# Source one-hots of the second gather stage: from one wide VectorE compare to ScalarE distances and a rectifier

## The chip, the cores and the metric

One core of a Trainium2 chip runs the whole program. The metric is the device time of one execution in microseconds (us). The times are those of the kernel before and after on the same kind of core; a profile is one execution of its own.

## What is computed

The reference takes 6250 nodes with 256 values and 100000 edges (src, dst). What matters here is the graph layer and what stands behind it:

```
xn = layernorm(x)
agg = segment_sum(xn[nbr], dst, 6250); cnt = segment_sum(1, dst, 6250)
x = x + (xn @ W1.T + b1 + (agg / max(cnt, 1)) @ W2.T + b2) + mix(xn)     # mix: per head of 32: q @ (k^T v / N), k and v normalized xn
x = x + ffn(layernorm(x))                                                 # 8 experts, one per node, capacity 977
```

(The call passes edge_index = stack(src, dst), so rows are summed by src and fetched by dst.)

## The kernel before, in words

The edges are sorted on the chip into tiles of 128 edges, by block of 128 nodes. For each tile, GpSimd's L511 issues one indirect DMA, which gathers 128 rows of 1 KB (a high and a low fp16 part of the projected node) out of the DRAM tensor xn_parts into a ring of 32 slots (the SBUF tensor w). TensorE then sums a tile into nodes by two matmuls (L764 with the high part and a column of ones, L765 with the low part) against a one-hot matrix S of 128 edges by 128 nodes: S[p, n] = 1 where edge p belongs to node n of the block. VectorE's L1018 adds the PSUM result to the block's sums in XA.

There are two gather stages. The first has T0 = 392 tiles, one block each; beside it the second chunk of edges is sorted (VectorE and ScalarE). The second stage has 438 dense tiles; a tile that holds a boundary between blocks is summed once for each block, which makes 486 items. The queues in it:

- GpSimd (L502 to L512) has nothing but gathers. For a gather of the second stage it waits until SyncE says that the slot 32 tiles back is free (s_free, L469); SyncE says so when the last item of that tile was summed.
- SyncE (L459 to L469) counts landed tiles (s_land, L461), and TensorE waits for that count before an item (L758).
- TensorE: `sum_tile(t)` (L743) waits for the landing, at each eighth item for the one-hots (s_S), and for the adding of the item four back (s_ev). Between items stand the products of the heads (L826; items 16 to 287, behind VectorE and ScalarE steps that `heads` orders), and, from item 288 on, one "own" part for each of 49 blocks, four items apart: transposes (L838), then products with W1 and the bias (L844, L846).
- VectorE: `tile(t)` (L1003) adds an item (L1018). The one-hots of eight tiles are one instruction, `source_onehots` (L995 to L999), half a group ahead. S has 16 tiles, so two groups. Between items stand the head statistics (L1301 to L1322), `key_values` (L1327) ahead of item 288, and the two additions of each own block (L1361, L1364).
- ScalarE (L599 to L627): Square and Sqrt for each of 17 head batches (L601, L603), then for each own block a copy of XA (L620, which TensorE's transposes wait for), a copy of the transposes (L623), and a DMA of x (L613).

The block ends when all queues are through; then come `nodes` (L1378, normalization, routing, scatter to expert rows) and `experts` (L1625).

The line that the change takes out of the second stage:

```
v.tensor_tensor(S[:, ...8 tiles...], iota_1 (broadcast over 8 tiles), srcl[:, t:t + SB] (broadcast over 128 nodes), ALU.is_equal)
```

Of the kernel before, what the change touches and what calls it, by code (L numbers as in the profile page):

```python
# [5 lines left out]
ALU = mybir.AluOpType  # L6
ACT = mybir.ActivationFunctionType
AX = mybir.AxisListType
F32 = mybir.dt.float32
F16 = mybir.dt.float16  # L10
# [6 lines left out]
P = 128  # L17
N, D = 6250, 256
NB = -(-N // P)
LASTROWS = N - (NB - 1) * P  # L20
LD = 4
HD = 3
# [16 lines left out]
SR, SB = 16, 8  # L39
AR = 4  # L40
KR, KR1 = 8, 12
# [32 lines left out]
T0 = CHUNKS[0][3]  # L74
DENSE = -(-COLS1 * EP // P)
ITEMS = DENSE + NB - 1
IW = -(-ITEMS // SB) * SB
AHEAD = 16
WMAX = max(c[1] for c in CHUNKS)
TMAX = max(T0, IW)  # L80
# [5 lines left out]
HEAD0, KV_AT = 1, 1 + NB // HD + 1  # L86
OWN0 = KV_AT
# [156 lines left out]
def edges(nc, ctx, kk, dram, x, src, dst, w1t, w2t, gb1, gb2, kw, kb, vw, vb, gate_w, gate_b):  # L244


    def sb(name, shape, dt):
        return ctx.enter_context(nc.sbuf_tensor(name, shape, dt))

    def sem(name):  # L250
        return ctx.enter_context(nc.semaphore(name))
# [3 lines left out]
    XA, ident, upper, upinc, ones, eps = (kk[n] for n in ("XA", "ident", "upper", "upinc", "ones", "eps"))  # L255
    W1, W2, brow, gw, gb = (kk[n] for n in ("W1", "W2", "brow", "gw", "gb"))
    bank = kk["psum"]
    psV, psP, psG, psQ = bank[2:4], bank[4], bank[5:7], bank[7]
# [12 lines left out]
    iota_1 = sb("iota_1", [P, P], F16)  # L271
# [39 lines left out]
    LH = sb("LH", [P, KR * P], F16)  # L311
    LV = sb("LV", [P, KR * 2 * P], F16)
    HT = sb("HT", [P, KR * TMAX], F16)
# [5 lines left out]
    assert KR1 == KR + 4 and LB == 4 and 12 * P + 4 * TMAX <= 4 * LD * D  # L319
    DI = HT[:, :].bitcast(I32)  # L320
    idx = sb("idx", [P, T0 + CHUNKS[1][3]], I32)
    srcl = sb("srcl", [P, T0 + IW], F16)
    buck = sb("buck", [1, T0 + IW], I32)
    lanes = sb("lanes", [P, 6], F32)
    starts = sb("starts", [P, 4], F32)
# [3 lines left out]
    keep = v2[:, 0:IW // 2].bitcast(F16)  # L329
# [5 lines left out]
    pick = [HT[:, n * TMAX:n * TMAX + IW] for n in range(4)]  # L335
    assert IW // 2 <= COLS0 and CHUNKS[1][3] <= 4 * P and IW // 2 <= EC - IW
    S = sb("S", [P, SR * P], F16)
    xT = [S[:, n * 4 * D:(n + 1) * 4 * D].bitcast(F32) for n in range(2)]
    spare = [G2[:, n * GW:n * GW + 2 * D] for n in range(GR)]
    hv = sb("hv", [P, 2 * 2], F32)  # L340
# [24 lines left out]
    s_S, s_tile, s_ev = sem("source_onehot"), sem("tile_summed"), sem("tile_added")  # L365
# [13 lines left out]
    s_past = sem("past_a_wait")  # L379
    s_ts, s_tr, s_trc, s_si, s_sid, s_rows = (sem(n) for n in (  # L380
        "sources_by_lane", "sources_turned", "sources_by_tile", "sources_picked", "item_sources", "item_rows_ready"))
    s_land, s_free = sem("tiles_landed"), sem("tiles_free")

    block = ctx.enter_context(nc.Block())
# [130 lines left out]
    def _(act):  # L515
# [80 lines left out]
                ins = act.activation(value_slot(k, n), lane_slots(k, 1), ACT.Copy, scale=v[0:EP, COLS0 + k:COLS0 + k + 1])  # L596
            ins.then_inc(s_lv, 1)

        def heads(m, nb):  # L599
            act.wait_ge(s_cen, m + 1)  # L600
            act.activation(sqr[:, 0:nb * D], cen[:, 0:nb * D], ACT.Square).then_inc(s_sq, 1)  # L601
            act.wait_ge(s_ss, m + 1)
            act.activation(hq[:, 0:nb * HEADS], hq[:, 0:nb * HEADS], ACT.Sqrt, scale=1.0 / (HC - 1)).then_inc(s_hstd, 1)  # L603
        with act.Fori(0, NB // HD) as m:
            heads(m, HD)
        heads(NB // HD, 1)
        act.wait_ge(s_kv, 1)

        def again(b):
            if b >= LD:  # L610
                act.wait_ge(s_x0, b - LD + 1)
            rows = P if b < NB - 1 else LASTROWS
            act.dma_start(xr[b % LD][0:rows, :], x[b * P:b * P + rows, :]).then_inc(s_xr[b % LD], 16)  # L613

        for b in range(2):
            again(b)

        def own(b, h):
            act.wait_ge(s_xt, b + 1)
            act.activation(xs[:, h * D:(h + 1) * D], XA[:, xcols(b)], ACT.Copy).then_inc(s_xs, 1)  # L620
            act.wait_ge(s_xt, b + 3)
            act.wait_ge(s_xp, b + 1)
            act.activation(xts[:, h * D:(h + 1) * D], psV[h][:, 0:D], ACT.Copy).then_inc(s_xtc, 1)  # L623
        for b in range(NB):
            own(b, b % 2)
            if b + 2 < NB:
                again(b + 2)  # L627

    @block.tensor
    def _(pe):  # L630
# [112 lines left out]
        def sum_tile(t):  # L743
            if t == 0:
                pe.wait_ge(s_one, 2)
            if t < T0:
                o = slot(t)
                pe.wait_ge(s_g[t % RING], 16 * (t // RING + 1))
            else:
                i = t - T0  # L750
                if i % GR == 0:
                    many = min(GR, ITEMS - i)
                    item[:] = [nc.values_load_multi_w_load_instructions(
                        row[:, i:i + many], engines=[mybir.EngineType.PE], min_val=low, max_val=high,
                        skip_runtime_bounds_check_because="an item's tile is one of the DENSE tiles, its slot one of the ring")[1]
                        for row, low, high in ((item_slot, 0, (RING - 1) * GW), (item_need, 1, DENSE))]
                o = item[0][i % GR]
                pe.wait_ge(s_land, item[1][i % GR] & 511)  # L758
            if t % SB == 0:
                pe.wait_ge(s_S, t // SB + 1)  # L760
            if t >= AR:
                pe.wait_ge(s_ev, t - AR + 1)
            lhs = S[:, t % SR * P:(t % SR + 1) * P]
            pe.matmul(psA[t % AR][:, 0:AGW], lhs, ring_high[:, ds(o, AGW)], start=True, stop=True)  # L764
            pe.matmul(psA[t % AR][:, 0:D], lhs, ring[:, ds(o, D)], start=False, stop=True, skip_group_check=True).then_inc(s_tile, 1)  # L765
# [109 lines left out]
    def _(v):  # L875
# [83 lines left out]
        n = NB // (2 * LD)  # L959
# [43 lines left out]
        def tile(t):  # L1003

            if (t if t < T0 else t - T0) % GR == 0:
                many = min(GR, (T0 if t < T0 else T0 + ITEMS) - t)
                offsets[:] = nc.values_load_multi_w_load_instructions(
                    buck[0:1, t:t + many], engines=[mybir.EngineType.DVE], min_val=0, max_val=(NB - 1) * RW,
                    skip_runtime_bounds_check_because="the place step clamps the tiles' blocks to NB - 1")[1]
            if t in (0, T0):  # L1010
                source_onehots(t)
            if t % SB == SB // 2 and t + SB // 2 not in (T0, T0 + IW):
                source_onehots(t + SB // 2)
            v.wait_ge(s_tile, t + 1)
            if t:
                v.wait_ge(s_ev, t)
            o = offsets[(t if t < T0 else t - T0) % GR]
            v.tensor_tensor(XA[:, ds(o, AGW)], XA[:, ds(o, AGW)], psA[t % AR][:, 0:AGW], ALU.add).then_inc(s_ev, 1)  # L1018
# [151 lines left out]
        def decode_dense():  # L1170

            tiles = CHUNKS[1][3]
            v.wait_ge(s_sx, 2)
            a, b, d, e = (DI[:, n * TMAX:n * TMAX + tiles] for n in range(4))
            v.tensor_copy(a, psV[0][:, 0:tiles])
            step(v.tensor_copy(b, psV[1][:, 0:tiles]))
            v.memset(lane_src[:, tiles:4 * P], 0.0)
            v.tensor_copy(ident16, ident[:, :])
            wait()
            v.tensor_scalar(d, a, 3, None, ALU.logical_shift_left)  # L1180
            step(v.tensor_scalar(e, b, 8, None, ALU.logical_shift_right))
            wait()
            step(v.tensor_scalar(a, b, 255, None, ALU.bitwise_and))
            v.tensor_tensor(idx[:, T0:T0 + tiles], d, e, ALU.bitwise_or).then_inc(s_dec, 1)
            wait()
            v.tensor_copy(lane_src[:, 0:tiles], a).then_inc(s_ts, 1)
            for _ in range(GAP):
                yield
            v.wait_ge(s_ts, 1)
            for n in range(4):  # L1190
                v.tensor_scalar(pick[n], item_tile, lanes[:, 2 + n:3 + n], None, ALU.is_equal)
            v.wait_ge(s_tr, 1)
            v.tensor_copy(src_lane, psG[0][:, 0:4 * P]).then_inc(s_trc, 1)
            step(v.tensor_scalar(item_slot, item_tile[0:1, :], float(1 + T0 % RING), None, ALU.add))
            v.tensor_scalar(item_need, item_tile[0:1, :], 2.0, None, ALU.add)
            v.tensor_copy(tile_used, used16[0:1, :])
            wait()
            step(v.tensor_scalar(item_slot, item_slot, RING - 1, None, ALU.bitwise_and))
            wait()
            step(v.tensor_scalar(item_slot, item_slot, float(GW), None, ALU.mult))  # L1200
            for _ in range(GAP):
                yield
            wait()
            v.sem_inc(s_rows, 1)
            v.wait_ge(s_si, 1)
            v.tensor_tensor(srcl[:, T0:T0 + IW], psG[1][:, 0:IW], keep, ALU.mult).then_inc(s_sid, 1)
            v.wait_ge(s_sid, 1)

        after_mask = {16: lambda: pair_stats(0), 24: lambda: pair_scale(0), 28: largest,
# [149 lines left out]
        def own(b):  # L1359
            v.wait_ge(s_xp, b + 3)  # L1360
            v.tensor_tensor(XA[:, xcols(b)], XA[:, xcols(b)], psG[b % 2][:, 0:D], ALU.add).then_inc(s_xa, 1)  # L1361
            v.wait_ge(s_xr[b % LD], 16 * (b // LD + 1))
            v.wait_ge(s_xa, b + 3)
            v.tensor_tensor(XA[:, xcols(b)], XA[:, xcols(b)], xr[b % LD], ALU.add).then_inc(s_x0, 1)  # L1364
# [465 lines left out]
```

## Time and profile before

| what | us |
|---|---|
| median of 3 runs (lowest to highest) | 1998.8 (1995.85 to 1999.64) |
| the profiled execution's own time | 1998.75 |
| its span, first to last instruction | 1997.1 |
| first gather of the first stage (L511) | 305 |
| first gather of the second stage | 836.57 |
| last gather | 1412.93 |
| first instruction of `nodes` | 1421.83 |

Busy time is a share of the span over stages with different limits. Engines: PE is TensorE, PEld its weight loads, DVE VectorE, ACT ScalarE, POOL GpSimd, SPq SyncE's queue. PEclk is the granted clock of TensorE as a share of full speed. A busy POOL in a gather is GpSimd writing the descriptors of one indirect DMA, and not the transfer.

### The profile page before, as it was taken

How to read it: one execution, taken by the hardware profiler on the slowest of the kernel's cores; microseconds unless marked ns; L12 is line 12 of the kernel's file. 1: busy time of each engine (PE TensorE's matmuls, PEld its weight loads, DVE VectorE, ACT ScalarE, POOL GpSimd, SP SyncE). 2: the span in 40 equal slices, each digit the busy share in tenths (PEclk: the TensorE clock that was granted, in tenths of full speed). 3: DMA queues.
4: the chain of work that ended last, by engine and by line, in shares of the span. 5: the costliest groups of instructions: out<-in, count | busy, mean ns of one | idle time of the engine just before them, and what ended most of it. 6: DMA issues, size and time to landing. Idle time of an engine off the chain costs nothing. (4 is left out here: it accounts for less than half of the span.)

```text
span 1997.1 us, 27369 instructions
## 1 busy us (share of the span) xinstructions
PE 1529.7 (77%) x6558; PEld 885.3 (44%) x6558; DVE 1367.3 (68%) x3735; ACT 710.2 (36%) x1954; POOL 985.5 (49%) x969
## 2 busy tenths in 40 slices
PE   4599995667778777365665558798593999999997
PEld 2255542233333333133333335454482766666665
DVE  8998997889998988476666657666781433444344
ACT  4488890008787876000000002111281222222221
POOL 0000006777777777777777777777263111111111
PEclk7699997679999998555555558878655999999999
DMA  6980013333333333743333334444464123323200
GB/s 185 180 151 32 32 36 86 98 100 94 99 98 97 95 96 98 86 123 100 101 100 101 98 111 131 127 132 127 140 226 163 41 96 97 105 96 103 101 9 5
DMA packets 101500, 204.49 MB, mean 102 GB/s; under 512 B 19794, under 2 KB 64760, under 8 KB 99392
## 3 DMA queue, kind: packets, MB, share of 16 engines
q0 software_dynamic: 49488, 131.52, 23.6%
q1 hardware_dynamic: 43164, 64.16, 12.1%
q10 hardware_dynamic: 8700, 7.07, 1.2%
q8 instruction: 64, 1.05, 0.2%
q14 instruction: 84, 0.69, 0.1%
HBM read 157.43 MB, written 49.89 MB: 104 GB/s over the span
## 5 line engine op out<-in xcount | busy, mean ns | idle before, releaser
L511 POOL DMA_INDIRECT w<-xn_parts,idx x830 | 856.4, 1032 | 260.8 <-issue 236.4
L1018 DVE TENSOR_TENSOR XA<-XA,bank 128x257 f32 x878 | 367.3, 418 | 280.9 <-PE bank L765 250.1
L764 PE MATMUL bank<-w,S 128*128 (+1 forms) x878 | 294.0, 337 | 275.0 <-SPq L461 114.6
L764 PEld LDWEIGHTS bank<-w,S 128*128 128x128 f16 x878 | 93.4, 106 | 486.8 <-issue 301.1
L765 PE MATMUL bank<-w,S 128*128 (+1 forms) x878 | 298.2, 342 | 0.0
L1800 POOL DMA_INDIRECT out<-ob,tok x64 | 66.5, 1040 | 401.2 <-DVE ob L1786 384.9
L596 ACT ACTIVATE LV<-LH,v 125x128 f16<-125x128 f16 x600 | 182.5, 388 | 195.8 <-DVE LH L1268 195.5
L1724 PE MATMUL bank<-w,ht 128*117 128x256 f32 (+1 forms) x1024 | 223.7, 379 | 0.0
L1713 PE MATMUL bank<-xt,w 128*128 128x468 f32 (+1 forms) x512 | 214.8, 578 | 0.8 <-ACT xt L1738 0.8
L1748 ACT ACTIVATE ht<-bank,b1c 128x468 f32<-128x468 f32 (+1 forms) x128 | 85.6, 669 | 333.4 <-PE bank L1713 333.4
L1724 PEld LDWEIGHTS bank<-w,ht 128*117 128x117 f32 (+1 forms) x1024 | 188.8, 186 | 30.5 <-issue 0.4
L1777 DVE TENSOR_TENSOR y<-bank,b 128x256 f32<-128x256 f32 (+1 forms) x64 | 27.1, 424 | 234.5 <-PE bank L1724 234.4
L731 PE MATMUL bank<-HT,LV 125*128 125x440 f16 x600 | 151.5, 361 | 15.6 <-ACT LV L596 12.5
L489 POOL DMA_DIRECT2D xn_parts<-w x13 | 10.7, 826 | 281.4 <-DVE w L953 281.4
L1713 PEld LDWEIGHTS bank<-xt,w 128*128 128x128 f32 x512 | 97.9, 191 | 109.1 <-issue 106.6
L997 DVE TENSOR_TENSOR S<-iota,srcl 128x1024 f16<-128x1024 f16 x110 | 133.9, 1217 | 2.2 <-issue 2.2
L601 ACT ACTIVATE work<-work 128x768 f32<-128x768 f32 (+1 forms) x17 | 13.9, 817 | 330.5 <-DVE work L1307 330.5
L765 PEld LDWEIGHTS bank<-w,S 128*128 128x128 f16 x878 | 94.8, 108 | 33.9 <-issue 10.0
L590 ACT ACTIVATE LV<-LH,v 125x128 f16<-125x128 f16 x354 | 108.0, 391 | 3.0 <-DVE LH L1237 3.0
L596 ACT ACTIVATE work<-work,v 125x128 f16<-125x128 f16 x296 | 90.4, 388 | 24.7 <-DVE work L1268 24.5
L1273 DVE TENSOR_SCALAR HT<-iota_t,tf 125x440 f16<-125x440 f16 x300 | 94.9, 343 | 0.0
L725 PE MATMUL bank<-HT,LV 125*128 125x392 f16 x354 | 80.2, 336 | 11.3 <-ACT LV L590 6.7
(290 smaller groups left out, 2326.0 us busy)
## 6 DMA issues: line engine op xcount, KB each, us to landing
w<-f SPq DMA_DIRECT2D x16, 1024.0 KB, 7.6
w<-xn_parts,idx POOLq DMA_INDIRECT x830, 2.8
expert_rows<-XA SPq DMA_DIRECT2D x2, 6296.5 KB, 62.7
xb<-expert_rows SPq DMA_DIRECT2D x8, 1028.0 KB, 11.4
xb<-expert_rows SPq DMA_DIRECT2D x8, 939.7 KB
XA<-x SPq DMA_DIRECT2D x6, 1024.0 KB, 5.6
xn_parts<-w POOLq DMA_DIRECT2D x12, 512.0 KB, 3.3
work<-x ACTq DMA_DIRECT2D x48, 128.0 KB, 2.2
```

The costliest lines, as they stand in the source:

```text
L511: pool.indirect_dma_start(ring[:, o:o + 2 * D], None, tab, bass.IndirectOffsetOnAxis(ap=idx[:, t:t + 1], axis=0)).then_inc(s_g[t % RING], 16)
L590: ins = act.activation(value_slot0(col, n), lane_slots0(col, 1), ACT.Copy, scale=v[0:EP, col:col + 1])
L596: ins = act.activation(value_slot(k, n), lane_slots(k, 1), ACT.Copy, scale=v[0:EP, COLS0 + k:COLS0 + k + 1])
L731: ins = pe.matmul(psV[n][:, 0:CHUNKS[1][3]], value_slot(k, n), tile_slot(k), start=False, stop=False, skip_group_check=True)
L764: pe.matmul(psA[t % AR][:, 0:AGW], lhs, ring_high[:, ds(o, AGW)], start=True, stop=True)
L765: pe.matmul(psA[t % AR][:, 0:D], lhs, ring[:, ds(o, D)], start=False, stop=True, skip_group_check=True).then_inc(s_tile, 1)
L997: v.tensor_tensor(S[:, t % SR * P:(t % SR + SB) * P].rearrange("p (j n) -> p j n", n=P), iota_1[:, :].unsqueeze(1).to_broadcast([P, SB, P] ...
L1018: v.tensor_tensor(XA[:, ds(o, AGW)], XA[:, ds(o, AGW)], psA[t % AR][:, 0:AGW], ALU.add).then_inc(s_ev, 1)
L1273: v.tensor_scalar(tile_slot(k + j), iota_t[0:EP, 0:tiles], tf[0:EP, k + j:k + j + 1], None, ALU.is_equal).then_inc(s_ht, 1)
L1713: ins = pe.matmul(psH[f % 2][:, 0:cols], w1[q][:, k * F + f * P:k * F + (f + 1) * P], xt[n % 2][:, k * TQ * P:k * TQ * P + cols], start=(k ...
L1724: ins = pe.matmul(psY[m % 2][0:rp, 0:D], ht[:, f * TQ * P + m * rp:f * TQ * P + (m + 1) * rp], w2[q][:, f * D:(f + 1) * D], start=(f == 0) ...
L1748: act.activation(ht[:, f * TQ * P:f * TQ * P + cols], psH[f % 2][:, 0:cols], ACT.Relu, bias=b1c[:, e * FT + f:e * FT + f + 1]).then_inc(s_ ...
```

## The change

In the second stage the one-hots of a group of eight tiles are made by ScalarE: eight activations with Abs (iota_1 minus the tile's source, as a bias per partition, 128 columns each) into a buffer `far` in LH, four at a time, and one activation with Relu of 1 - |distance| over 1024 columns into S. VectorE writes the negated sources once, as fp32, in place of the fp16 ones (L1206). ScalarE's queue is written out anew: head steps, own steps, the half groups of distances and the one-hots alternate. The first stage keeps VectorE's one-hots.

```diff
+        def distances(j, half):
+            if j >= S1_GROUPS:
+                return
+            if half == 0 and j:
+                act.wait_ge(s_S1, j)
+            for n in range(half * SB // 2, (half + 1) * SB // 2):
+                ins = act.activation(far[:, n * P:(n + 1) * P], iota_1[:, :], ACT.Abs,
+                                     bias=less_src[:, j * SB + n:j * SB + n + 1])
+            ins.then_inc(s_far, 1)
+        def onehots(j):
+            if j >= S1_GROUPS:
+                return
+            act.wait_ge(s_far, 2 * j + 2)
+            act.wait_ge(s_tile, T0 + (j - 1) * SB)
+            o = (T0 // SB + j) * SB % SR * P
+            act.activation(S[:, o:o + SB * P], far, ACT.Relu, bias=ones[:, 0:1], scale=-1.0).then_inc(s_S1, 1)
-        with act.Fori(0, NB // HD) as m:
-            heads(m, HD)
-        heads(NB // HD, 1)
-        act.wait_ge(s_kv, 1)
-        for b in range(2):
-            again(b)
-        for b in range(NB):
-            own(b, b % 2)
-            if b + 2 < NB:
-                again(b + 2)
+        act.wait_ge(s_sid, 1)
+        for j in range(2):
+            distances(j, 0)
+            distances(j, 1)
+            onehots(j)
+        for g in range(max(S1_GROUPS // 2, OWN0 + -(-NB // LD))):
+            m, nb = g - HEAD0, HD if g - HEAD0 < NB // HD else 1
+            if g == KV_AT:
+                act.wait_ge(s_kv, 1)
+                for b in range(2):
+                    again(b)
+            for r in range(LD):
+                if HEAD0 <= g < KV_AT and r < 2:
+                    (squares, roots)[r](m, nb)
+                b = (g - OWN0) * LD + r
+                if g >= OWN0 and b < NB:
+                    own(b, b % 2)
+                    if b + 2 < NB:
+                        again(b + 2)
+                distances(2 * g + 2 + r // 2, r % 2)
+                if r % 2:
+                    onehots(2 * g + 2 + r // 2)
...
             if t % SB == 0:
-                pe.wait_ge(s_S, t // SB + 1)
+                if t < T0:
+                    pe.wait_ge(s_S, t // SB + 1)
+                else:
+                    pe.wait_ge(s_S1, (t - T0) // SB + 1)
...
-            if t in (0, T0):
+            if t == 0:
                 source_onehots(t)
-            if t % SB == SB // 2 and t + SB // 2 not in (T0, T0 + IW):
+            if t % SB == SB // 2 and t + SB // 2 < T0:
                 source_onehots(t + SB // 2)
...
-            v.tensor_tensor(srcl[:, T0:T0 + IW], psG[1][:, 0:IW], keep, ALU.mult).then_inc(s_sid, 1)
+            v.scalar_tensor_tensor(out=less_src, in0=psG[1][:, 0:IW], scalar=-1.0, in1=keep, op0=ALU.mult,
+                                   op1=ALU.mult).then_inc(s_sid, 1)
```

`squares` and `roots` are the two halves of the old `heads`; `own` and `again` are unchanged. There are 61 groups.

## Rows read from the trace of the kernel before

**Rows 1.** The page: busy time of each engine, and GpSimd's in 40 slices

```profile
PE 1529.7 (77%) x6558; PEld 885.3 (44%) x6558; DVE 1367.3 (68%) x3735; ACT 710.2 (36%) x1954; POOL 985.5 (49%) x969
...
POOL 0000006777777777777777777777263111111111
```

**Rows 2.** Windows: heads' part and own part of the second stage

```profile
core 0: us, PE busy (x) PEld busy (x) DVE busy (x) ACT busy (x) POOL busy (x), PEclk, DMA share, GB/s
860.00:1176.00 316.00, 190.03 (x744) 104.01 (x744) 211.03 (x432) 17.66 (x34) 243.18 (x240) 0.56 0.35 100
...
1192.00:1417.00 225.00, 190.44 (x788) 114.17 (x788) 141.57 (x320) 38.67 (x97) 170.81 (x169) 0.80 0.44 128
```

**Rows 3.** The chain that ended last: where it starts (start us, us, what)

```profile
1530.25 0.55 SPq L1666
```

**Rows 4.** Waits, 830 to 1420 us: GpSimd's (total, times, longest)

```profile
POOL w L511 <- SPq L469: 3.7, 12, 0.3
```

**Rows 5.** Line L511, 836 to 1414 us (duration ns min/median/max)

```profile
L511 POOL DMA_INDIRECT w<-xn_parts,idx x439: 942/946/1992, 835.3 to 1412.9; - x147
```

**Rows 6.** Timeline: end of the second stage (start us, us, what)

```profile
1412.93 1.06 POOL L511 DMA_INDIRECT w<-xn_parts,idx  x1 [0.30 <-issue]
...
1416.80 0.42 DVE L1018 TENSOR_TENSOR XA<-XA,bank 128x257 f32 x1 [0.39 <-PE bank L765]
1421.83 0.39 SPq L166 DMA_DIRECT2D w<-f  x1
```

**Rows 7.** Line L997, VectorE's one-hots, 836 to 1414 us

```profile
L997 DVE TENSOR_TENSOR S<-iota,srcl x61: 1215/1218/1283, 854.1 to 1406.8; 128x1024 f16<-128x1024 f16 x61
```

**Rows 8.** Timeline: one gather beside L1322, one beside L997

```profile
1002.39 0.95 POOL L511 DMA_INDIRECT w<-xn_parts,idx  x1 [0.30 <-issue]
1002.64 0.95 DVE L1322 TENSOR_TENSOR work<-work,hr 128x768 f32<-128x768 f32 x1
...
1005.35 1.22 DVE L997 TENSOR_TENSOR S<-iota,srcl 128x1024 f16<-128x1024 f16 x1
...
1006.15 1.25 POOL L511 DMA_INDIRECT w<-xn_parts,idx  x1 [0.30 <-issue]
```

**Rows 9.** Timeline: first and last of 65 slow gathers beside an L997

```profile
858.48 1.22 DVE L997 TENSOR_TENSOR S<-iota,srcl 128x1024 f16<-128x1024 f16 x1
...
859.08 1.45 POOL L511 DMA_INDIRECT w<-xn_parts,idx  x1 [0.30 <-PE bank L765]
...
1406.83 1.22 DVE L997 TENSOR_TENSOR S<-iota,srcl 128x1024 f16<-128x1024 f16 x1
1406.92 1.95 POOL L511 DMA_INDIRECT w<-xn_parts,idx  x1 [0.30 <-issue]
```

**Rows 10.** Groups by form, 860 to 1400 us (busy, mean ns | idle before, releaser)

```profile
L620 ACT ACTIVATE work<-XA 128x256 f32<-128x256 f32 x47 | 19.6, 417 | 20.6 <-DVE mcol L1357 20.4
L1364 DVE TENSOR_TENSOR XA<-XA,work 128x256 f32<-128x256 f32 x45 | 19.2, 426 | 5.0 <-DVE XA L1361 0.5
...
L1322 DVE TENSOR_TENSOR work<-work,hr 128x768 f32<-128x768 f32 x16 | 15.2, 953 | 0.0
L1307 DVE TENSOR_TENSOR work<-XA,hm 128x768 f32<-128x768 f32 x16 | 15.2, 951 | 0.0
...
L601 ACT ACTIVATE work<-work 128x768 f32<-128x768 f32 x16 | 13.5, 843 | 316.2 <-DVE work L1307 316.2
...
L601 ACT ACTIVATE work<-work 128x256 f32<-128x256 f32 x1 | 0.4, 416 | 14.2 <-DVE work L1307 14.2
```

**Rows 11.** Windows: 100 us of the first stage, columns as in Rows 2

```profile
500.00:600.00 100.00, 78.75 (x421) 35.27 (x420) 92.50 (x251) 80.72 (x268) 77.44 (x75) 0.98 0.35 99
```

**Rows 12.** Timeline: start of the second stage's sums

```profile
854.08 1.25 DVE L997 TENSOR_TENSOR S<-iota,srcl 128x1024 f16<-128x1024 f16 x1 [0.74 <-issue]
...
855.53 0.39 PE L764 MATMUL bank<-w,S 128*128 x1 [1.89 <-SPq L461]
```

**Rows 13.** TensorE's waits, 1200 to 1400 us (total, times, longest)

```profile
PE bank L764 <- SPq L461: 21.5, 25, 2.3
```

More of the change, by code:

```diff
@@ L321, in edges @@
     idx = sb("idx", [P, T0 + CHUNKS[1][3]], I32)
-    srcl = sb("srcl", [P, T0 + IW], F16)
+    srcl = sb("srcl", [P, T0], F16)
     buck = sb("buck", [1, T0 + IW], I32)
@@ L337, in edges @@
     S = sb("S", [P, SR * P], F16)
+    less_src = HT[:, 4 * TMAX:4 * TMAX + 2 * (IW)].bitcast(F32)
+    far = LH[:, 0:SB * P]
+    S1_GROUPS = (IW) // SB
+    assert 2 * (IW) <= 4 * TMAX and SB <= KR and T0 % SB == 0
     xT = [S[:, n * 4 * D:(n + 1) * 4 * D].bitcast(F32) for n in range(2)]
@@ L381, in edges @@
         "sources_by_lane", "sources_turned", "sources_by_tile", "sources_picked", "item_sources", "item_rows_ready"))
+    s_S1, s_far = sem("source_onehot_second"), sem("source_distances")
     s_land, s_free = sem("tiles_landed"), sem("tiles_free")
@@ L597, in _, with squares, roots @@
             ins.then_inc(s_lv, 1)
-        def heads(m, nb):
+        def distances(j, half):
[14 more added lines that the diff above has]
+            act.activation(S[:, o:o + SB * P], far, ACT.Relu, bias=ones[:, 0:1], scale=-1.0).then_inc(s_S1, 1)
+        def squares(m, nb):
             act.wait_ge(s_cen, m + 1)
             act.activation(sqr[:, 0:nb * D], cen[:, 0:nb * D], ACT.Square).then_inc(s_sq, 1)
+        def roots(m, nb):
             act.wait_ge(s_ss, m + 1)
             act.activation(hq[:, 0:nb * HEADS], hq[:, 0:nb * HEADS], ACT.Sqrt, scale=1.0 / (HC - 1)).then_inc(s_hstd, 1)
-        with act.Fori(0, NB // HD) as m:
-            heads(m, HD)
-        heads(NB // HD, 1)
-        act.wait_ge(s_kv, 1)
         def again(b):
```

## The prediction

> **What bounds the kernel now.** I read the page first, then the stage in windows, then GpSimd's waits and its line. The page says that no engine is busy throughout, and that GpSimd is busy in 77% of each slice over all of the two gather stages, flat, with one dip [rows 1]. A flat level under 100% is the sign of an engine with a fixed pause between instructions. The chain that ended last starts only at 1530 us, in `experts` [rows 3], so it says nothing of the gather stage; but the stages are in blocks that follow one another, and whatever the gather stage's end gains, all behind it gains. So the question is what ends the gather stage. Its last gather starts at 1412.93, the last sum is added at 1416.80, and `nodes` begins at 1421.83 [rows 6]: the stage ends 3.9 us after its last gather starts, which is little more than one landing and one item.
>
> GpSimd issues the 438 gathers without a break. Its longest wait for a free slot is 0.3 us, and that is also the pause between any two gathers, so it is never really held [rows 4, 6]. A gather takes 0.946 us in the median and at least 0.942, but up to 1.99 [rows 5]. 438 gathers at 0.946 + 0.30 would take 546 us; from 836.57 to 1412.93 they took 576. The 30.7 us between are gathers that were stretched. So the second stage is bound by GpSimd's descriptor writing, and the only thing in it that can be saved is these 30.7 us.
>
> Where do they come from? I went through the timeline gather by gather beside VectorE's. 74 gathers took over 1.00 us, and 65 of them overlap an L997, with 27.7 of the 30.7 us. The first is at 859.08 (1.45 us, L997 at 858.48), the last at 1406.92 (1.95 us, L997 at 1406.83) [rows 9]; a gather beside an fp32 instruction such as L1322 keeps its 0.95 us while one that meets the L997 at 1005.35 takes 1.25 [rows 8]. The windows agree without any pairing: 860 to 1176 holds 240 gathers in 243.18 us, 16.1 above 240 x 0.946, and the own part 169 in 170.81, 10.9 above [rows 2]. What is left, 3.0 us, lies beside L1322, L1364 and the like.
>
> **The change part by part.** *Removed from VectorE:* 61 one-hots of 1.218 us, 74.4 us [rows 7]. As VectorE's own time this is worth nothing: VectorE is busy 211 of 316 us and 142 of 225 [rows 2], and it isn't what ends the stage. What it is worth is the stretching: 27.7 us, or 0.454 us for each of the 61. The lowest bound is 0, if whatever replaces L997 stretches the gathers as much; the highest is all of 30.7.
>
> L997 is not the only VectorE instruction with two inputs in SBUF: L1322, L1307 and L1364 have 49.6 us of such time beside its 74.4 [rows 7, 10]. The rows speak for L997 alone, so the sum goes by 27.7; an even blame is rival 2. The page "GPSIMD Engine Reference" of the Trainium skill (8. Key points) stands for the even blame: GpSimd shares its SBUF interfaces with VectorE and contends with every VectorE instruction that runs in a two-port mode or has two SBUF inputs. By it the time would be that of rival 2, about 1982, and not 1973.
>
> *Added to ScalarE:* for each group eight activations of 128 columns and one of 1024. The near row for the former is the sorting's activations of 125 x 128 fp16 with a scale per partition, 268 in 80.72 us, 0.301 each back to back [rows 11]; eight are 2.4 us. For the latter the two forms of L601 give (843 - 416)/512 = 0.834 ns for a column and 1.06 us for 1024 [rows 10]. Both ends: 3.5 us for a group, and if the eight don't overlap and the three waits in a group cost 0.3 us each, 8 x 0.39 + 1.06 + 0.9 = 5.1 (0.39 is my estimate from 0.416 for 256 columns, less the 107 ns of 128 columns, and a margin of 80). A group's time will be 8/486 of about 549 us, 9.0 us. ScalarE's other work in the own part is 38.67 us in 225 [rows 2], 1.5 us a group. That makes 5.0 to 6.6 of 9.0: it fits, and no sum has a term for it. ScalarE works beside GpSimd in the first stage also, and 75 gathers took 77.44 us in 100 us with 80.72 of ScalarE's busy time [rows 11], 6.5 above 75 x 0.946, 0.087 for each, against 0.067 in the heads' part with ScalarE nearly idle (16.1 for 240), and VectorE has the fp16 compares of the sorting beside L997 there; and no gather of the second stage that met ScalarE alone took over 0.95.
>
> *Table loads:* Copy, Square and Sqrt already alternate in this stage without one, and Relu and Copy do in `experts`. I put 0. If Abs needed another table than Sqrt, 34 loads would lie in the heads' part, where ScalarE has 298 of 316 us free [rows 2]; the cover is large.
>
> *The first group comes later.* L997 at 854.08 let the first item start at 855.53 [rows 12]. Now 2.4 + 1.1 us on ScalarE stand there in place of 1.25, so the first item starts some 2.3 us later. Ahead of GpSimd lie 32 slots, and it is at gather 16 of the stage then; the lag is caught up before it needs slot 33. Price 0.
>
> *The order in ScalarE's queue.* This is the edit that can cost. The one-hots of group j + 1 wait until group j - 1 is all summed, and in the own part the next block's copy (L620, 0.417 us [rows 10]) stands behind them in the queue; TensorE's transposes wait for that copy, one item later. So once in every eight items TensorE may be held: Relu 1.06 + copy 0.42 + some 0.1, 1.6 us after the eighth item, less the item between. If TensorE is waiting for landings anyway, the next item ends some 1.4 us later and the stall is 0.2; if it has a backlog, the item takes 0.4 and the stall is 1.2. Does it have room? In the own part (24 groups) it is busy 190.4 of 225 us [rows 2] and waits 21.5 of 200 us for landings [rows 13], 24 over the part. The faster gathers take 10.9 of these, so 13 are left, 0.55 for a group, against a stall of 0.2 to 1.2. In the same part the adds no longer queue behind L997. Then there is `key_values`: ScalarE waits 20.4 us for it [rows 10], some 15 gathers pile up, and TensorE has the own part to work them off at a smaller surplus than now. I expect that it nearly does: I put the stage's end 2 us later behind its last gather than now, with 0 and 10 as the ends (10 being ten items not yet caught up at about 1 us each).
>
> *The conversion* at L1206 is one instruction for one. 0.
>
> **The sum.** On the profiled execution, 1998.75 (span 1997.1 and 1.65 around it; the median of the runs is 1998.8, the same): -27.7 for the gathers, +2 for TensorE's lag at the end: **1973.0 us**.
>
> **The rivals.**
> 1. *TensorE becomes the bound of the own part.* For it: busy 85%, and a stall that is 1.2 us a group once it lags, against 0.55 of room. The granted clock is 0.80 there [rows 2], so part of its work runs at 1.2 GHz, and stalls could keep it there. Against: a TensorE that lags is busy without a gap, and has finished its pile by 1250 us in this trace. If the own part doesn't get faster at all, its 10.9 us stay: 1982 to 1984. 17%.
> 2. *The stretching belongs to all VectorE instructions with two SBUF inputs alike*, and those that stay keep theirs, or take over what L997 had. L997 has 74.4 of 124.0 us of such time [rows 7, 10], 60%; 60% of 30.7 is 18.4, so 1998.75 - 18.4 + 2 = 1982. Against it are gathers of 0.95 us beside L1322 [rows 8]. 8%.
> 3. *Nothing moves*: ScalarE's reads and writes of fp16 stretch the descriptors as VectorE's did; 1998. Against it is the whole first stage. 3%.
> 4. *Slower: ScalarE's queue sets the pace of the own part.* One mechanism: Relu, the block's copy and the waits between stand in series with TensorE's transposes. The own part takes 225/24.75 = 9.1 us a group of eight now, with 7.7 of TensorE's work. The heads' part still gains 16 us, or 0.65 a group of the own part, so it decides from 9.75 on: from a stall of over 2.0 us a group. At 3 us, when distances too stand ahead of the copy, it is 10.7, 265 us for 225, 40 lost and 16 + 1 won: about 2022. 5%.
>
> My forecast has 67%, from 1969 to 1979. The range takes in the first two rivals: **1967 to 1984**. Faster by over 0.2% (4 us, about what a measurement can tell here): 0.92; within 0.2%: 0.03; slower: 0.05.
>
> **What the profile after would show.** The gathers of the second stage at 0.30 + 0.946 us, about 3 us above in all, the last starting near 1385; GpSimd still never held. No L997 behind 836 us, VectorE's share down by 74 us. ScalarE's eight near 2.4 us and Relu near 1.06. TensorE's transposes in the own part waiting for L620, some 0.2 to 1.2 us once in eight items, and the stage's last add 4 to 8 us behind the last gather. Everything from `nodes` on as long as before (1421.83 to the end, 575 us). It would be wrong if gathers are still stretched (rivals 2 and 3), or if the last gather starts on time but the last add comes over 10 us behind it, or GpSimd waits for slots (rivals 1 and 4).

## The result and the profile after

The changed kernel takes 1993.01 us (median of 20 runs, 1987.11 to 2000.83), the kernel before 1998.07 (20 runs): ratio 0.9974, 95% interval 0.9964 to 0.9984. It is faster by a quarter of a percent, where 1.3% was forecast; 1993 lies outside the forecast range of 1967 to 1984. The profiled execution took 1994.81, its span is 1993.2, and 575.8 us of it lie behind the gather stages as before (575.3). So what there is to explain lies in the second gather stage.

The page of the kernel after, against [rows 1]: VectorE has 62 us less, ScalarE 213 us more, and in slice 29 of 40 (1395 to 1445 us), where the stage ends, GpSimd is down from 2 to 0: its gathers are done before.

```profile
PE 1540.6 (77%) x6558; PEld 891.4 (45%) x6558; DVE 1305.0 (65%) x3674; ACT 922.9 (46%) x2503; POOL 964.0 (48%) x969
...
POOL 0000006777777777777777777777063111111111
```

The groups by form, 860 to 1410 us: what the one-hots cost ScalarE (busy us, mean ns). Four distances take 1.28 us back to back, the rectifier 1.15 (1.06 was worked out).

```profile
L611 ACT ACTIVATE LH<-iota,HT 128x128 f16<-128x128 f16 x456 | 143.2, 388 | 1.1 <-DVE XA L1407 0.3
...
L622 ACT ACTIVATE S<-LH,ones 128x1024 f16<-128x1024 f16 x58 | 66.6, 1148 | 131.8 <-PE bank L807 131.2
```

The window of the kernel after for the heads' part, columns as in [rows 2]:

```profile
860.00:1176.00 316.00, 193.01 (x748) 107.53 (x748) 177.10 (x404) 136.83 (x341) 241.38 (x246) 0.54 0.35 103
```

The heads' part has 246 gathers in 316 us for 240 before. For the own part I take the same work in each kernel, from the start of item 288 to that of item 480: the kernel before, the kernel after, and the one with the moved copy that is told of below.

```profile
1192.83:1410.52 217.69, 186.42 (x768) 112.00 (x769) 137.40 (x309) 38.28 (x96) 167.43 (x166) 0.79 0.44 129
...
1181.92:1411.18 229.26, 198.40 (x768) 118.73 (x769) 113.36 (x285) 118.37 (x303) 159.82 (x168) 0.75 0.43 125
...
1182.37:1392.36 209.99, 180.24 (x769) 108.59 (x770) 112.27 (x285) 115.60 (x303) 159.11 (x168) 0.82 0.47 135
```

The own part is 11.6 us longer than before, and TensorE is busy 12.0 us longer with the same matmuls, at a granted clock of 0.75 in place of 0.79. TensorE's waits in the kernel after, 1192 to 1410 us (total, times, longest):

```profile
PE bank L880 <- ACT work L640: 22.2, 22, 1.4
...
PE bank L806 <- SPq L466: 0.4, 1, 0.4
```

Over items 288 to 480 the kernel before has 23.4 us of waits for landings (in 200 us of it they are the 21.5 of [rows 13]). They are gone but for 0.4, and 22.2 us of waits for ScalarE's copy (L640) before the transposes (L880) are there: GpSimd isn't what TensorE waits for any more. All of TensorE's waits over 0.15 us add up to 37.8 us before and 37.5 after. So the stalls took the place of the waits for landings, and what lengthened the own part is the same matmuls at a lower clock: TensorE had 1.2 GHz, the lower of its two levels, for 115.1 us of it and for 90.4 before, and 24.7 us more at half the clock are 12.3 us of work. The end of the stage, against [rows 6]:

```profile
1391.67 0.95 POOL L516 DMA_INDIRECT w<-xn_parts,idx  x1 [0.30 <-issue]
...
1416.63 0.42 DVE L1060 TENSOR_TENSOR XA<-XA,bank 128x257 f32 x1
1417.33 0.39 SPq L166 DMA_DIRECT2D w<-f  x1
```

The stage in the profiles:

| us | before | after | moved copy (below) |
|---|---|---|---|
| first gather of the stage starts | 836.57 | 834.92 | 835.31 |
| from there to the last gather's start | 576.4 | 556.8 | 556.6 |
| from item 0 to item 276 (heads) | 313.2 | 307.6 | 306.2 |
| from item 288 to item 480 (own) | 217.7 | 229.3 | 210.0 |
| last gather's start to `nodes` | 8.9 | 25.7 | 8.8 |

The gathers gave 19.6 us. The stage's end, which now comes 25.7 us behind the last gather and not 8.9, gave 16.8 back. The stage also began 1.65 us sooner, so `nodes` starts 4.5 us sooner, and the span is 3.9 shorter.

### The profile page after: what moved, and what is told of

Read it like the earlier page. It is cut to its first block and busy times, and to the rows that moved or that the text cites. A ratio compares the mean times of both kernels' runs of the same rounds, so it can differ in the third digit from the quotient of the medians.

```text
span 1993.2 us, 27869 instructions
## 1 busy us (share of the span) xinstructions
PE 1540.6 (77%) x6558; PEld 891.4 (45%) x6558; DVE 1305.0 (65%) x3674; ACT 922.9 (46%) x2503; POOL 964.0 (48%) x969
## 5 line engine op out<-in xcount | busy, mean ns | idle before, releaser
L516 POOL DMA_INDIRECT w<-xn_parts,idx x830 | 834.8, 1006 | 260.8 <-issue 234.9
L611 ACT ACTIVATE LH<-iota,HT 128x128 f16<-128x128 f16 x488 | 153.0, 388 | 16.7 <-DVE HT L1248 15.6
L622 ACT ACTIVATE S<-LH,ones 128x1024 f16<-128x1024 f16 x61 | 70.0, 1148 | 173.8 <-PE bank L807 173.2
L601 ACT ACTIVATE work<-work,v 125x128 f16<-125x128 f16 x296 | 90.4, 387 | 23.3 <-DVE work L1311 23.1
```

Of the source, the lines that this page charges most:

```text
L516: pool.indirect_dma_start(ring[:, o:o + 2 * D], None, tab, bass.IndirectOffsetOnAxis(ap=idx[:, t:t + 1], axis=0)).then_inc(s_g[t % RING], 16)
L611: ins = act.activation(far[:, n * P:(n + 1) * P], iota_1[:, :], ACT.Abs, bias=less_src[:, j * SB + n:j * SB + n + 1])
```

## What held the gathers, row by row

Behind the result I paired every gather's start and length with VectorE's instructions more finely than in the forecast. Take the point 0.14 us after a gather's start. If a VectorE instruction with two inputs in SBUF runs at it, and began at least 0.18 us ahead of it (0.04 us ahead of the gather), the extra length of the gather is the end of that instruction less the point, within 0.02 us in all rows but one, which fits within 0.03. In the second stage of the kernel before, 66 gathers meet such an instruction with over 0.03 us still to run, and all are held. 9 more meet one that began 0.01 to 0.17 us ahead of the point (8 times L997), and none is lengthened. In the first stage 4 gathers are held by one that began so late, each time right behind an L1273 compare. Of the kernel after, a gather and the fp32 centring of the heads, no one-hot near:

```profile
1009.17 0.95 DVE L1350 TENSOR_TENSOR work<-XA,hm 128x768 f32<-128x768 f32 x1
1009.33 1.60 POOL L516 DMA_INDIRECT w<-xn_parts,idx  x1 [0.30 <-issue]
```

The instruction ends at 1010.12, the point is 1009.47, the hold 0.65: 0.946 + 0.65 is 1.60. The same sum gives, to 0.03 us, the 1.25 us of the gather at 1006.15 in [rows 8] (1006.57 less 1006.29 is 0.28), the 1.45 and the 1.95 of [rows 9], and it gives nothing for the gather at 1002.39 beside L1322, since that begins 0.25 us after the gather. Counted so, L997 holds 44 gathers of the kernel before by more than 0.03 us, for 20.1 us in all, L1307 12 gathers for 7.0, L1322 1.4, L1364 0.8. L1307 stood close ahead of L997, and the gather of both had been put down to L997. In the kernel after, 10.4 us are left of 30.1, 8.1 of them with the centring. Every gather there that is over 0.98 us long has a VectorE instruction at its point, so ScalarE's distances and rectifiers, new in this stage, hold none; that answers rival 3.

## The experiments

All kernels are changed from the kernel after (or before, where said), and each ratio is to the kernel before on the same chip. They ran on five chips. On one the kernel before took 1998.19 us, as in the first measurements. On the four others it took 2169 to 2187 us. There engines pause between instructions that nothing separates: in the kernel with the moved copy, 0.73 us from L811 to L812 of one item, where in the first profile of the kernel before no pair has over 0.28 us in 900 to 1250 us, and here 17 have 0.7 or more (start us, us, what).

```profile
1111.59 0.37 PE L811 MATMUL bank<-w,S 128*128 x1 [2.55 <-issue]
...
1112.32 0.39 PE L812 MATMUL bank<-w,S 128*128 x1 [0.36 <-issue]
...
1112.54 0.94 POOL L516 DMA_INDIRECT w<-xn_parts,idx  x1 [2.37 <-SPq L474]
```

GpSimd then is held by slots that aren't free (its pauses in the second stage add up to 226 to 249 us there, to 133 on the others), and gathers don't set the pace. I call them the slow chips and tell both. What makes the pauses isn't known.

**The order of ScalarE's queue.** The copy of the next own block ahead of distances and one-hots; `own` loses its copy to `placed`:

```diff
+        def placed(b, h):
+            act.wait_ge(s_xt, b + 1)
+            act.activation(xs[:, h * D:(h + 1) * D], XA[:, xcols(b)], ACT.Copy).then_inc(s_xs, 1)
...
                     if b + 2 < NB:
                         again(b + 2)
+                    if b + 1 < NB:
+                        placed(b + 1, (b + 1) % 2)
                 distances(2 * g + 2 + r // 2, r % 2)
```

> The changed kernel, with one thing moved in ScalarE's queue: the copy of the next own block (which TensorE's transposes wait for) stands ahead of the distances and the one-hots, and not behind them. Theory Q (the order of ScalarE's queue holds TensorE in the own part, 22 us of waits before the transposes): these waits vanish, the own part is bound by landings again, the last gather still starts about 557 us after the stage's first, and the stage ends 8 us behind it: about 15 us less than the changed kernel, 1976 to 1980. Rival C (TensorE itself is the bound there, its work at a granted clock of 0.76; the waits only take the place of idle time): the waits vanish, but the own part is at most 5 us shorter, 1988 to 1993.

Measured on a slow chip: 2191.88 us, 1.0021 (1.001 to 1.0033). With no control beside it this decided nothing, so both were run on another.

> The changed kernel again, as the control for the others of this call, since the chip of the first call took 2187 us for the kernel before, 9% more than the chip of the first measurements, with pauses before instructions of all engines that those don't show. On a chip like the first: 0.997 of the kernel before. On one like the second, by theory Q, the one-hots have more to wait for in either place: about the same as the kernel before, 0.999 to 1.003.

> The kernel with the own block's copy ahead of the distances, beside its control. Theory Q: TensorE's waits for that copy fall from 22 us to under 3 and, where gathers set the pace, the kernel is 10 to 17 us below the changed kernel (ratio to before 0.988 to 0.992). Rival C: within 5 us of the changed kernel.

The changed kernel: 2203.86 us, 1.0081 (1.0065 to 1.0097), slower than before. The moved copy: 2188.87, 1.0004 (0.9993 to 1.0015). Between them 15.0 us (14.9 in the profiles); of these the own part's items 288 to 480 show 7.3 (264.1 and 256.8 us), and 4.6 lie ahead of the second stage, where the two don't differ. TensorE's waits don't vanish here: those before the transposes fall from 36.7 us to none, but those before the products with W1 rise from 3.3 to 37.9. The difference is again in TensorE's busy time for the same items, 216.2 and 205.9 us at clocks of 0.67 and 0.71. Then, on the chip where gathers set the pace:

> The changed kernel once more, as a control on this call's chip: 0.997 of the kernel before where that takes 1998 us, 1.008 where it takes 2187.

> The own block's copy ahead of the distances, once more beside its control. Theory Q: 10 to 17 us below the control. If the kernel before takes 1998 us here, that is 0.988 to 0.992 of it.

1990.47 us, 0.9968 (0.9953 to 0.9983), the first result again; and 1977.61, 0.9896 (0.9874 to 0.9917). Theory Q's time holds, rival C's doesn't. The moved copy's waits of TensorE, 1190 to 1410 us:

```profile
PE bank L811 <- SPq L466: 13.5, 18, 2.2
...
PE bank L891 <- ACT work L645: 4.9, 8, 0.7
```

The wait for the copy of XA (L640) isn't among them (L645 is the copy of the transposes), that for landings is back, and `nodes` starts 8.8 us behind the last gather's start, as before:

```profile
1391.87 0.95 POOL L516 DMA_INDIRECT w<-xn_parts,idx  x1 [0.30 <-issue]
...
1400.66 0.39 SPq L166 DMA_DIRECT2D w<-f  x1
```

Rival C is right in part, though. In items 288 to 480 all waits of TensorE over 0.15 us are 37.5 us in the kernel after and 36.3 with the copy moved, so the copy's waits had indeed only taken the place of others. Of the 19.3 us between the two, 18.2 are TensorE's busy time (198.4 and 180.2 us), at clocks of 0.75 and 0.82: it has 1.2 GHz for 115.1 us in the one and 76.9 in the other. What rival C had wrong is that this clock would stay when the waits go. The control on this chip shows the changed kernel's clock again (0.75, 198.9 us busy, 229.8 us long). Why the clock is lower where the stalls stand before the transposes, no run here shows.

How one such wait comes about is in the kernel after: the rectifier begins when item 8k - 1 is summed, the copy stands behind it, and the transposes behind the copy.

```profile
1307.54 1.15 ACT L622 ACTIVATE S<-LH,ones 128x1024 f16<-128x1024 f16 x1 [0.95 <-PE bank L807]
...
1308.59 0.40 ACT L640 ACTIVATE work<-XA 128x256 f32<-128x256 f32 x1
...
1309.04 0.44 PE L880 MATMUL bank<-ident,work 128*128 128x128 f32 x2 [1.39 <-ACT work L640]
```

**The wait without the order.** A third group's room, so that the rectifier waits one group less:

```diff
+    S2 = [S[:, SB * P:2 * SB * P], S[:, 0:SB * P], mask[:, 2048:2048 + SB * P].bitcast(F16)]
...
-            act.wait_ge(s_tile, T0 + (j - 1) * SB)
+            act.wait_ge(s_tile, T0 + (j - (2 if j > 1 else 1)) * SB)
```

> The changed kernel with its queues in the same order, but the second stage's one-hots have room for three groups in place of two (the third in a buffer that is free by then), so that ScalarE's rectifier waits for the group before the last but one, and never for the item that TensorE has just made. It takes away the wait and leaves the order. Theory Q: the next own block's copy comes some 1.2 us earlier once in eight items, TensorE's waits before the transposes fall from 22 us to under 5, and the time is within 3 us of that of the kernel with the copy moved. Rival C: no more than 5 us below the changed kernel. If the order matters beyond the wait (rectifier and distances are 2.4 us of ScalarE ahead of the copy), it lies between.

> Room for three groups of one-hots and the changed kernel's order, once more, where gathers may set the pace. Theory Q, in the form that the wait on the item just made is what holds the copy: TensorE's 22 us of waits fall under 5 and the time is within 3 us of that with the copy moved ahead (0.989 to 0.991). If the 2.4 us of distances and rectifier ahead of the copy also hold, between that and 0.997.

> The third slot once more, in case gathers set the pace on this chip. Theory Q in the form of the wait: 0.989 to 0.991 of the kernel before, TensorE's waits before the transposes under 5 us. In the form of the order: between that and 0.997. Where the kernel before takes 2170 to 2187 us: the same as it, as twice before.

All three fell on slow chips: 2189.67 us, 1.0007 (0.9993 to 1.002); 2171.14, 1.0007 (0.9996 to 1.0019); 2173.16, 1.0006 (0.9994 to 1.0018). On slow chips the changed kernel has 1.0081 and the moved copy 1.0021 and 1.0004, so the third slot takes away all or nearly all of what the moved copy does, with the order as it was. In its three traces the waits before the transposes are 1.1 to 1.4 us in items 288 to 480, where the changed kernel has 36.7 on its slow chip, and those before the products with W1 are 28 to 42, near the moved copy's 38. That speaks for the wait on the item just made; where gathers set the pace it wasn't seen.

**One part of the stage alone.** VectorE's wide compare again for the groups outside ACT_LO to ACT_HI:

```diff
-            if j >= S1_GROUPS:
+            if not ACT_LO <= j < min(ACT_HI, S1_GROUPS):
                 return
...
+            if t % SB == SB // 2 and n not in (T0, T0 + IW) and not ACT_LO <= (n - T0) // SB < ACT_HI:
+                source_onehots(n)
```

> ScalarE makes the one-hots of groups 0 to 35 (up to the heads' part's end), VectorE's wide compare those of groups 36 to 60 (the own part). The wide compares that are back stretch gathers again, some 9 to 11 us, in the own part, but ScalarE's queue has nothing ahead of the block's copy. Theory Q: the heads' part keeps its gain (item 288 about 10 us earlier than in the kernel before), the own part takes what it took before (218 us from item 288 to 480), so about 10 us under the kernel before, 1987 to 1990, which is less than the changed kernel. Rival C says nearly the same of this one.

> ScalarE's one-hots for groups 0 to 35 alone, once more, where gathers may set the pace. The own part is VectorE's again, without the copy standing behind anything. Theory Q: holds of L997's kind in the own part cost about 9 us, those of the heads' part are gone (about 9 us): 9 us under the kernel before, 0.995 to 0.996. On a chip where the kernel before takes 2187 us: the same as it, as in the first call.

> The reverse: VectorE's wide compare for groups 0 to 35, ScalarE for 36 to 60. Theory Q: the heads' part gains nothing, and the own part's 10 us of spared stretching are more than eaten by the held transposes (229 us in place of 218 from item 288 to 480): slower than the kernel before, by 4 to 9 us, 2002 to 2007. Rival: if the own part were bound by landings also, 1988 to 1990.

ScalarE in the heads' part alone: 2188.21 us, 1.0004 (0.9992 to 1.0015), and 2171.28, 1.0012 (0.9999 to 1.0025), both on slow chips. In the own part alone: 2199.56, 1.007 (1.0057 to 1.0083). So the loss comes with the own part, with most of the 0.8% of the whole change there. The gain in the heads' part can't be seen on chips where gathers don't set the pace, and how it divides stays open but for the profiles' 5.6 us (313.2 less 307.6).

**The hold itself.** The wide compare of two inputs as eight compares against a scalar per partition, on VectorE, from the kernel before; in both stages, or (scalars2) the second alone. ScalarE's queue is the old one.

```diff
-            v.tensor_tensor(S[:, t % SR * P:(t % SR + SB) * P].rearrange("p (j n) -> p j n", n=P),
...
+            for n in range(SB):
+                o = (t % SR + n) * P
+                one = srcl[:, t + n:t + n + 1] if t < T0 else src2[:, t - T0 + n:t - T0 + n + 1]
+                ins = v.tensor_scalar(S[:, o:o + P], iota_1[:, :], one, None, ALU.is_equal)
+            ins.then_inc(s_S, 1)
```

> The kernel before, with each wide compare of the second stage (two inputs in SBUF) as eight compares of 128 columns against a per-partition scalar (one input), still on VectorE; ScalarE and its queue are as before. Theory H (a gather that begins while a VectorE instruction with two inputs in SBUF runs is held until that one ends, and one with one input holds it little): the 20.0 us that the wide compares hold in the second stage fall to under 3, eight short compares take some 1.4 us in place of 1.2, and the own part keeps its order: the stage ends about 17 us earlier, 0.991 to 0.993 of the kernel before. Rival W (VectorE's fp16 one-hots hold gathers in any form): within 5 us of the kernel before.

> As the one before, in both gather stages. Theory H: in the first stage the wide compares hold 26.9 us in 47 gathers, which fall to under 3 too; 40 to 44 us in all, 0.978 to 0.981 of the kernel before, unless the first stage's sorting becomes its bound (VectorE is busy 85% there), then 0.985. Rival W: within 5 us of the kernel before.

> One-hots by compares against per-partition scalars in both stages, once more. Where the kernel before takes 1998 us, by theory H 0.978 to 0.985 of it; where it takes 2187, the same as it, as in the call before.

On a slow chip 2186.86 us, 1.0007 (0.9994 to 1.0019), and 2187.58, 1.0 (0.999 to 1.001): nothing, although the holds fell. On the one where gathers set the pace 1954.86, 0.9787 (0.9767 to 0.9808), as theory H had it, and the fastest kernel of the study. Its compares are 0.25 us each and hold 0.4 us in all in the second stage; GpSimd's busy time by windows, second row the second stage, is 424.86 us for 438 gathers:

```profile
305.00:812.00 507.00, 387.05 (x392) 0.87 0.39 101
812.00:1370.00 558.00, 424.86 (x438) 0.67 0.42 117
```

The two stages of the kernel before have 411.81 us for 392 gathers and 444.55 for 439. One thing isn't separated: the scalar compares have one input, and they are also short. A compare against a scalar that is longer does hold gathers by the same relation: in the first stage of the kernel before L1273 (fp16, 440 columns, 0.33 us) holds 16 gathers for 1.5 us, by 0.17 us at most. Whether eight short compares with two inputs would do as well wasn't run.

**At a point or by time.** The centring done twice (in the kernel after), then cut in three (in the kernel before with the scalar compares):

```diff
-                v.tensor_tensor(cen[:, w].rearrange("p (j g d) -> p j g d", j=nb, d=HC), xb,
...
+                for j in range(nb):
+                    ins = v.tensor_tensor(cen[:, j * D:(j + 1) * D].rearrange("p (g d) -> p g d", d=HC),
...
+                ins.then_inc(s_cen, 1)
```

> The changed kernel with the centring of the heads (VectorE, fp32, 128 x 768, both inputs in SBUF, no one-hots) done twice, the second time with the same result. It tests which VectorE instructions hold gathers. Theory H (any instruction with two inputs in SBUF holds a gather that begins while it runs, until it ends): the 8 us that this line holds in the second stage become 12 to 16 us, each held gather ending with the instruction within 0.02 us. Rival W (only fp16 one-hots do it, and the line's 8 us are something else): unchanged at about 8 us or spread over other lines.

1997.03 us, one execution. The line holds 8.6 us, not 12 to 16. The expectation was worked out wrongly: after a hold a gather needs 0.80 us more, and the next one's point lies 1.25 us behind the end of the first centring, when the second (0.95 us) is over. In its timeline the gather of 1.62 us is held by the first of the two, and the next is free:

```profile
1012.09 1.94 DVE L1352 TENSOR_TENSOR work<-XA,hm 128x768 f32<-128x768 f32 x2
1012.23 1.62 POOL L516 DMA_INDIRECT w<-xn_parts,idx  x1 [0.30 <-issue]
...
1014.16 0.94 POOL L516 DMA_INDIRECT w<-xn_parts,idx  x1 [0.30 <-issue]
```

A hold that lasts as long as any such instruction runs would have made it 2.6 us (the pair ends at 14.03, 1.66 behind the point). That speaks for a point, and the cut asked it the other way:

> One-hots by compares against scalars in both stages, and the centring of the heads cut into three instructions of 256 columns (0.42 us each in place of 0.95). Theory P (a gather is vulnerable at one point, 0.14 us after its start; a VectorE instruction with two SBUF inputs that runs then holds it until that instruction ends, for the rest of the instruction and no longer): the longest hold by this line falls from 0.81 to 0.28 us, and its sum in the second stage from 8.7 us to 2 to 4, the time by 5 us against the uncut one (0.976 of the kernel before where that takes 1998 us). Rival T (the hold is in proportion to the total time of such instructions, in whatever pieces): unchanged at 8 to 11 us, since the pieces are 1.27 us for 0.95.

The holds of this line are 1.3 us, in pieces of 0.42 us (below the 2 to 4 expected), and the longest is 0.23. The 8.7 they were to be compared with are from a chip where gathers set the pace: on slow chips the uncut line holds 1.6 and 3.2 us in the kernels with the scalar compares (the second stage alone, and both), so the sum decides little. The longest single hold does more, 0.59 and 0.55 us there against 0.23 here: it falls with the length of the piece, as theory P has it. The time, on a slow chip, is 2172.49 us, 1.0013 (0.9999 to 1.0027), and says nothing.

> As the one before, and in the first stage the sorting's lane compares (two fp16 inputs, 125 x 512, in groups of four columns) as four compares against scalars. By theory P their 12 us of holds in the first stage fall to under 2: 0.970 to 0.972 of the kernel before where that takes 1998 us, unless VectorE's longer work beside the first stage (four short instructions for one) takes it back. By rival T too they fall, since these have one input.

> The version with scalars in all one-hot and lane compares and the centring cut, once more, in case gathers set the pace on this chip: by theory P 0.970 to 0.972 of the kernel before where that takes 1998 us, 0.975 if the longer work of VectorE beside the first stage takes some back; the same as the kernel before where that takes 2170 to 2187.

2173.14 us, 1.0011 (1.0 to 1.0023), and 2174.39, 1.0013 (0.9998 to 1.0027), on two slow chips. The lane compares' holds in the first stage, 9 us in the kernel without this edit on the same chip, fall to 0.6, and the stage's whole to 5.0. Whether they are worth 12 us where gathers set the pace wasn't seen.

## Why the prediction was wrong

*What bounds the kernel* was read rightly: on the first chip GpSimd's gathers, never waiting, at 0.946 + 0.30 us. Only the reading of the stage's end was loose (3.9 us from the last gather to the last add). `nodes` starts 8.9 us after the last gather starts, 5.0 behind the last add, so the block's end waits for more than that add (for what, no run shows); with the moved copy and with the scalars it is 8.8 again. In the kernel after it starts 0.7 us behind the last add, so TensorE could have been some 4 us later at no cost.

*"-27.7 for the gathers"* was mis-sized: 19.6 came. The step that failed is the pairing, "65 of them overlap an L997, with 27.7 of the 30.7 us". Overlap isn't cause where two suspects stand side by side: 7.0 us were L1307's, and they are still there as L1350's 8.1. The rule that was weighed and set aside, that of "GPSIMD Engine Reference" in the Trainium skill (8. Key points), that any VectorE instruction with two SBUF inputs contends, was right as to which instructions do, and its 18.4 us (rival 2) was nearer than mine. The counter-example against it, L1322 beside an unheld gather, began after the vulnerable point. The rows agree with the page: where such an instruction began early enough it held every gather, and L1018, whose second input is in PSUM, held none by more than 0.1 us. What the page doesn't say is the point, by which L1322 holds 1.4 us and L1307 7.0 for the same length.

*"+2 for TensorE's lag"* was the larger fault. The mechanism was named, with a stall of 0.2 to 1.2 us a group, and measured 22.2 us in 22 waits, 1.0 each. But it was taken for something that the surplus would nearly absorb. The forecast's own account didn't allow it: a room of 0.55 us a group against 1.2 once there is a backlog, and `key_values` makes a backlog just ahead. TensorE then never catches up: its waits for landings fall from 23.4 us to 0.4. That alone would have left the own part at its old length, which is rival 1. But the forecast also took TensorE's own work there as fixed, at 190.4 us of 225. For the same items it grew by 12.0 us (186.4 to 198.4), at a granted clock of 0.75 in place of 0.79, with no more waiting than before. Rival 1 had named this ("stalls could keep it there") and priced it at nothing. So the own part took 229.3 us in place of 217.7, the last gather stood 25.7 us ahead of `nodes` in place of 8.9, and 16.8 us were gone. It isn't rival 4: the stalls are 0.9 us a group, and that needed over 2.0. Moving one copy of 0.4 us, 49 times, brings 13 to 15 us back on both kinds of chip.

Right were ScalarE's load (it fits, 118 of 229 us in the own part), the table loads (none more: 11 in either trace), the first group's price (none; item 0 even starts 5.1 us sooner and not 2.3 later, since ScalarE's first rectifier ends at 835.1 us, where L997 stood at 854.08), and everything from `nodes` on.

Not foreseen at all: on chips where engines pause, the change is 0.8% slower. There gathers don't set the pace, so what it gives is worth nothing, and what it costs stays.

## What to carry to other kernels

When work moves to an idle engine, ask first what stands behind it in that engine's queue and who waits for that: an instruction that waits for the newest item must not stand ahead of a copy that the next item needs. Before a stretching is put down to an instruction, look for one time relation that gives each row's length, and not for overlap. Where an engine's waits only change their cause, compare its busy time for the same items, and its clock. And where a contention with two-input instructions is the price, change the form of the instruction (fewer inputs, shorter pieces) before its engine: the scalar compares gave 43 us on the engine where the work already was (in both stages; from the second stage's first gather to its last they take 557.4 us for 576.4, some 19 of the 43), the move to ScalarE, in the second stage alone, 5 to 8.

## What the runs showed of the hardware

An indirect DMA of GpSimd (0.946 us for 128 rows) is held if a VectorE instruction with two inputs in SBUF, fp16 or fp32, began before it (0.04 us or more ahead in the rows of the second stage) and still runs 0.14 us after the gather's start; it goes on when that one ends and takes 0.80 us more. 43 of L997's 44 held gathers, L1307's 12 and L1364's 6 fit within 0.02 us, and the 9 gathers beside an instruction that began later than that weren't held. VectorE instructions that read one input in PSUM (L1018) or compare against a scalar hold a few gathers by some 0.1 us. In the second stage the longest hold is about the instruction's length less 0.18 us: 0.23 us for pieces of 0.42, and at most 0.08 for the scalar compares of 0.25.

TensorE's 768 matmuls of items 288 to 480 took 180, 186 and 198 us of busy time at granted clocks of 0.82, 0.79 and 0.75, with 36 to 38 us of waits in all three kernels.

The same program took 1998 us on some chips and 2169 to 2187 on four others, with pauses of 0.7 and 1.4 us between neighbouring instructions; of the 200 us only 12 lie behind the last item (590.2 us from its start to the end in the changed kernel, 578.6 in the first profile). An edit can have another sign there: 0.9968 and 1.0081 for the same kernel.
